# Graph attention kernel: steps of four single edge rows instead of two pairs, and landed data marked by VectorE

## The reference, cut to what matters

```python
x_l = (x @ W_l).reshape(n, 8, 16)
x_r = (x @ W_r).reshape(n, 8, 16)
e = (edge_attr @ W_e).reshape(-1, 8, 16)
m = leaky_relu(x_l[src] + x_r[dst] + e, 0.2)
alpha = einsum('ehc,hc->eh', m, att)
amax = segment_max(alpha, dst)
expa = exp(alpha - amax[dst])
denom = segment_sum(expa, dst)
out = segment_sum(x_l[src] * (expa / (denom[dst] + 1e-16))[:, :, None], dst)
```

## Time and profile before

| | |
|---|---|
| median of 3 runs | 2233.2 us (2232.06 to 2237.89) |
| the profiled execution's own time | 2248.54 us |
| its span | 2246.7 us |
| tables stage | 0 to about 52 us |
| gathers of the attention | 846.3 us to about 2126.5 us |
| last work of the attention | about 2185.2 us |
| granted TensorE clock, mean of the span | 0.864 |

### The profile page before, as it was taken

One profiled execution on the slowest core, in us unless ns is written; L12 is line 12 of the kernel. 1 busy time (PEld: TensorE's weight loads), 2 busy tenths in 40 slices (PEclk: granted clock), 3 DMA queues, 4 the chain that ended last, 5 costly groups with the idle time before them and its releaser, 6 DMA issues. The chain is left out here.

```text
span 2246.7 us, 35285 instructions
## 1 busy us (share of the span) xinstructions
PE 1820.9 (81%) x10692; PEld 1277.1 (57%) x10692; DVE 1327.8 (59%) x3113; ACT 1066.6 (47%) x2345; POOL 847.4 (38%) x891
## 2 busy tenths in 40 slices
PE   6777799979999973677878878878888778888776
PEld 2667665567888741345545555545555545555564
DVE  6999777664333363755555555555555555555585
ACT  1889867545423450234434444434444444444465
POOL 2000000010000016766666666666666666666500
PEclk9555599989999996799898998888989998999887
DMA  3000000005300012323233223323233233323311
GB/s 104 24 2 1 8 2 1 5 25 151 91 1 6 1 44 69 90 77 82 77 80 83 78 80 82 82 76 84 77 81 81 77 81 82 83 76 82 79 35 29
DMA packets 132195, 133.01 MB, mean 59 GB/s; under 512 B 28888, under 2 KB 102063, under 8 KB 132015
## 3 DMA queue, kind: packets, MB, share of 16 engines
q1 hardware_dynamic: 104238, 73.55, 11.4%
q0 software_dynamic: 27776, 57.20, 10.3%
HBM read 125.84 MB, written 4.82 MB: 58 GB/s over the span
## 5 line engine op out<-in xcount | busy, mean ns | idle before, releaser
L2275 POOL DMA_INDIRECT rows<-x_l,src x856 | 821.3, 959 | 477.1 <-issue 224.3
L2400 ACT ACTIVATE bent<-psum 128x512 f32<-128x512 f32 x214 | 127.4, 596 | 606.6 <-DMA near<-e_ends 340.6
L2361 PE MATMUL psum<-both,node_hot 128*128 128x144 f32 x1712 | 308.6, 323 | 66.3 <-issue 56.0
L2361 PEld LDWEIGHTS psum<-both,node_hot 128*128 128x128 f32 x1712 | 265.9, 213 | 143.0 <-issue 127.2
L2548 DVE TENSOR_TENSOR acc<-acc,psum 128x144 f32 x428 | 127.0, 297 | 278.4 <-remote 198.3
L2293 PEld LDWEIGHTS psum<-hot,x_r_parts 128*128 x1284 | 133.5, 104 | 249.0 <-issue 228.6
L2293 PE MATMUL psum<-hot,x_r_parts 128*128 128x256 bf16 x1284 | 201.2, 296 | 90.3 <-DVE hot L2454 31.1
L2415 ACT ACTIVATE apart<-iota,rel 128x128 bf16<-128x128 f32 x856 | 270.6, 388 | 1.4 <-PE psum L2361 1.4
L2313 PE MATMUL psum<-bent,att_heads 128*128 128x512 f32 x428 | 244.7, 661 | 9.0 <-DVE bent L2458 6.1
L2296 PE MATMUL psum<-edges,w_e 128*128 128x512 f32 x428 | 239.5, 642 | 0.7 <-issue 0.7
L2458 DVE TENSOR_TENSOR bent<-psum,bent 128x512 f32<-128x512 f32 x214 | 146.9, 686 | 127.9 <-issue 117.8
(11 more groups left out here) (347 smaller groups left out, 2400.3 us busy)
## 6 DMA issues: line engine op xcount, KB each, us to landing
rel_row<-e_rel_rows SPq DMA_DIRECT2D x107, 256.0 KB
edges<-edge_t SPq DMA_DIRECT2D x428, 32.0 KB
rows<-x_l,src POOLq DMA_INDIRECT x856
edge_part<-edge_t SPq DMA_DIRECT2D x40, 320.0 KB, 3.1
new<-e_new_before SPq DMA_DIRECT2D x26, 64.0 KB
new<-e_new_behind SPq DMA_DIRECT2D x26, 64.0 KB
ht<-x SPq DMA_DIRECT2D x6, 256.0 KB, 2.8
x_l<-rows SPq DMA_DIRECT2D x4, 320.0 KB
```

Source lines behind the costliest of these rows:

```text
L2275: e.indirect_dma_start(rows[:, g % ring, j * ROW:(j + 1) * ROW], None, k.xl, bass.IndirectOffsetOnAxis(ap=src[:, at:at + 1], axis=0)).then ...
L2361: final = e.matmul(to, near_hot[:, at, j, :], both[:, at, j, :], start=j % 2 == 0, stop=j % 2 == 1)
```

## The change

A piece of work is one row of 128 edges, a group is four rows, each with its own block. A row that lies in two blocks is taken twice: (806 + 24) / 4, rounded up, = 208 groups.

```diff
-        self.groups = -(-(self.pairs + self.nb - 1) // 2)
+        self.groups = -(-(self.tiles + self.nb - 1) // 4)
...
-EDGE_SLOTS = 3
+EDGE_SLOTS = 6
```

TensorE, `begin`, `join`, `turn_weights` and `sum_rows`:

```diff
-                    for j in range(2):
-                        half = slice(j * 2 * P, (j + 1) * 2 * P)
+                    for j in range(4):
+                        quarter = slice(j * P, (j + 1) * P)
                         for q in range(3):
-                            e.matmul(z[:, half], ...blocks[j]..., hot[:, two, half], start=j + q == 0, stop=False)
-                    e.wait_ge(edge_here[g % edge_slots].sem, edge_here[g % edge_slots].at(edge_lap(g)))
+                            e.matmul(z[:, quarter], ...blocks[j]..., hot[:, two, quarter], start=j + q == 0, stop=False)
                     e.matmul(z, w_e[:, :], edges[:, g % edge_slots, :], ...).then_inc(*products.up())
...
-                    e.wait_ge(got[g % slots].sem, got[g % slots].at(4 * lap(g)))
+                    e.wait_ge(seen.sem, seen.at(g + 1))
...
-                    if b.i >= 2:
-                        e.wait_ge(weighted.sem, weighted.at(plan[b.i - 2].over))
-                        e.wait_ge(filled.sem, filled.at(plan[b.i - 2].over))
+                    if b.i:
+                        e.wait_ge(weighted.sem, weighted.at(plan[b.i - 1].over))
+                        e.wait_ge(filled.sem, filled.at(plan[b.i - 1].over))
...
                     for j in range(4):
-                        to = bank[:, j // 2 * wide:(j // 2 + 1) * wide]
-                        final = e.matmul(to, near_hot[:, at, j, :], both[:, at, j, :], start=j % 2 == 0, stop=j % 2 == 1)
+                        row = 4 * u + j
+                        m, third = divmod(row, 3)
+                        bank = sum_banks[m % 3]
+                        if m >= 3 and third == 0:
+                            e.wait_ge(added.sem, added.at(adds(3 * m - 7)))
+                        ...
+                        final = e.matmul(bank[:, third * wide:(third + 1) * wide], near_hot[:, at, j, :], both[:, at, j, :],
+                                         start=True, stop=True)
```

SP and GpSimd:

```diff
-                        e.wait_ge(products.sem, products.at(g - edge_slots + 1))
-                    for j, at in enumerate(two):
-                        e.dma_start(...two rows of edge features...)
+                        e.wait_ge(leaky.sem, leaky.at(g - edge_slots + 1))
+                    for j, at in enumerate(four):
+                        e.dma_start(...one row of edge features...)
...
-                        e.wait_ge(joined.sem, joined.at(g - slots + 1))
+                        e.wait_ge(seen.sem, seen.at(g - slots + 1))
```

VectorE (`see(t + 1)` stands right behind `one_hots(t + 2)`; `see(0)` ahead of the loop):

```diff
                 def one_hots(g):
+                    e.wait_ge(edge_here[g % edge_slots].sem, edge_here[g % edge_slots].at(edge_lap(g)))
...
+                def see(g):
+                    e.wait_ge(got[g % slots].sem, got[g % slots].at(4 * lap(g)))
+                    e.tensor_copy(spot[:, g % 2:g % 2 + 1], rows_at(g)[:, 0:1]).then_inc(*seen.up())
...
-                    for j, to in enumerate(blocks):
-                        e.wait_ge(added.sem, added.at(adds(u) - 2 + j))
-                        e.tensor_tensor(to, to, bank[:, j * wide:(j + 1) * wide], ALU.add).then_inc(*added.up())
+                    for m in trios(u):
+                        bank = sum_banks[m % 3]
+                        e.wait_ge(totals.sem, totals.at(u + 1))
+                        for row in range(3 * m, min(3 * m + 3, 4 * groups)):
+                            to = acc[...the row's block...]
+                            ...
+                            e.wait_ge(added.sem, added.at(adds(row) - 1))
+                            e.tensor_tensor(to, to, bank[:, row % 3 * wide:(row % 3 + 1) * wide], ALU.add).then_inc(*added.up())
```

More of the change, by code:

```diff
@@ L537, in tables @@
         new_ready, stored = k.flag("new_ready"), k.flag("stored")
[L539 to L540 removed]
+        turns = [(srct, 0, 4, srcf), (relt, 0, 4, rel), (srct, 4, en, srcf), (relt, 4, en, rel)]
+        assert 4 < en <= 8 and len(c_cuts(s)) == 4
         ends_of = [(rowf, pair), (rows3, trio)]
         def turn(e, i):
[L544 to L546 removed]
+            _, lo, hi, of = turns[i]
+            for q in range(lo, hi):
+                last = e.transpose(k.bank[i][:, (q - lo) * P:(q - lo + 1) * P], of[:, q, :], k.ident[:, :])
             last.then_inc(*turned.up())
         def move(e, i):
[L550 removed]
+            to, lo, hi, _ = turns[i]
             e.wait_ge(turned.sem, turned.at(i + 1))
[L552 removed]
+            e.activation(to[:, lo * P:hi * P], k.bank[i][:, 0:(hi - lo) * P], ACT.Copy).then_inc(*moved.up())
         def turn_ends(e, i):
@@ L570, in _ @@
                 ended = groups.ends_of_tiles(e, v, c)
+                groups.find(e, v, c, ended, range(3))
                 c.vector_dst(e)
-                groups.vector(e, v, c, ended)
+                groups.find(e, v, c, ended, range(3, en))
+                groups.vector(e, v, c)
                 c.vector_src(e)
@@ L2139, in batch_of, with adds, trios @@
         return next(b for b in plan if b.first <= g < b.over)
-    def adds(u):
-        return 2 * (u + 1) + sum(b.first <= u for b in plan)
+    def adds(row):
+        return row + 1 + 2 * sum(4 * b.first <= row for b in plan)
+    def trios(u):
+        return [m for m in range(-(-4 * groups // 3)) if min(3 * m + 2, 4 * groups - 1) // 4 == u]
     def new_rows(b):
@@ L2205, in rows_at, with factors_in @@
             return rows[:, g % ring, :]
+        def factors_in(bank):
+            return bank[:, 3 * wide:3 * wide + HEADS]
         def weight_bank(b):
-            return k.bank[4 + b.two]
+            return k.bank[4]
         def turned_of(u):
@@ L2359, in sum_rows @@
                     for j in range(4):
-                        to = bank[:, j // 2 * wide:(j // 2 + 1) * wide]
-                        final = e.matmul(to, near_hot[:, at, j, :], both[:, at, j, :], start=j % 2 == 0, stop=j % 2 == 1)
+                        row = 4 * u + j
[3 more added lines that the diff above has]
+                            e.wait_ge(added.sem, added.at(adds(3 * m - 7)))
+                        if j == 0 and u in begun:
+                            i = begun[u].i
+                            e.wait_ge(spread.sem, spread.at(3 * i + 3))
+                            e.matmul(factors_in(bank), is_first[:, :], factor[:, :], start=True, stop=False)
+                            e.matmul(factors_in(bank), others[:, :], ones[:, :], start=False, stop=True).then_inc(*factors.up())
+                        final = e.matmul(bank[:, third * wide:(third + 1) * wide], near_hot[:, at, j, :], both[:, at, j, :],
+                                         start=True, stop=True)
                     final.then_inc(*totals.up())
                 e.wait_ge(loaded.sem, loaded.at(here))
-                block_of = Registers(k, ENGINE.PE, regs[0:1, 1, :], 2 * groups, s.nb - 1)
+                block_of = Registers(k, ENGINE.PE, regs[0:1, 1, :], 4 * groups, s.nb - 1)
                 begin(0)
@@ L2578, in _ @@
                 one_hots(1)
+                see(0)
                 def pieces(t, some):
@@ L2600, in _ @@
                         one_hots(t + 2)
+                    if t + 1 < groups:
+                        see(t + 1)
                     if t + 1 < cuts:
```

143 lines of the change are left out of this document (69 added, 74 removed).

## The result

The changed kernel takes 2525.62 us (median of 4 runs, 2520.41 to 2531.14), the kernel before 2234.78 us beside it: ratio 1.1299, interval 1.1272 to 1.1326. The prediction was 2082 us, range 1998 to 2270.

A forecast was written before the change was run, and what follows sets the result against it. It took late TensorE signals, binding both DMA-issuing engines, to set the attention's pace. From the profiled 2248.5 us, 157 less for the gathers, 3 more for the end and 2.5 for the tables gave 2097, scaled to 2082 us; range 1998 to 2270.

The forecast's parts named there:

- if the signals are prompt, the stops go: Attention gathers: GpSimd's wait moved to VectorE ends its 2 us stops; 5.40 us a group, 157 us less with fewer groups.
- Rival B: Attention: signals stay late, GpSimd restarts behind VectorE's queue, 1.53 us later at 100 stops, +153 us; 2355 us, chance 0.21.
- older piece of work: Argument against slower restarts: VectorE's copy runs one group ahead of the join, so GpSimd's wait may already be met.
- rival C: Attention gathers: GpSimd's floor of 5.06 us a group sets the pace, 227 us less; 2013 us, chance within the forecast's 0.52.
- TensorE: Attention: TensorE sets the pace at 5.28 us a group, including 0.66 for begin's twelve products.
- the theory of the signals: Attention: late TensorE signals, to which both DMA-issuing engines are bound, set the pace; moving the waits makes them prompt.
- Tables: Tables stage: SP's nine additional DMAs cost +2.5 us, from 0 to 7.6.
- End: After the last group: ten short steps follow instead of nine, +3 us.
- SP: Attention: two DMAs more a group stay hidden; without cover 1.2 us a group.
- the bank of weights: Attention: one bank makes turn_weights wait for the last weigh of the batch before; 0 to 28 us, taken as 0.
- factors: Attention: three banks of sums, factors of 8 columns, one additional VectorE operation a batch; 0, within 8 us either way.
- first steps: Attention's start: begin needs split x_r parts up to three steps earlier; 0 to 12 us, taken as 0.

The follow-up runs named there:

- e5: The changed kernel itself, unaltered, beside the kernel before, without late signals: 2022.9 us, ratio 0.993.
- e7: Kernel before, begin's six products of 256 columns made twelve of 128, four edge DMAs a group instead of two; not late: 2036.5 us, ratio 0.999.
- e1: Changed kernel with only GpSimd's wait undone, on TensorE's joined again; without late signals: 2021.1 us, kernel before 2039.6.
- e15: Changed kernel with all moved waits of GpSimd, SP and TensorE undone and no copy on VectorE; late signals: 2245.7 us, ratio 1.005.
- e10: Kernel before, GpSimd waiting for VectorE's copy, join held until the gathers six groups ahead land; late signals: 2713.8 us, ratio 1.207.
- e9: Kernel before, join in every second step held until the gathers five groups ahead land; late signals: 2427.6 us, ratio 1.080.
- the pause: A memset of 128 columns on GpSimd behind each gather: kernel before 2110.1 to 2115.1 us, changed kernel 2096.3 and, on joined, 2095.2 us.
- held kernels: Kernels before and changed, join made to wait for the landing of gathers five or six groups ahead: 2414.6 to 2813.9 us.
- e16: Changed kernel, GpSimd on joined again, join in every second step held for gathers five groups ahead; late signals: 2414.6 us, ratio 1.081.

## Why the prediction was wrong

**Failed: "if the signals are prompt, the stops go".** The term of the sum was 157 us less for the gathers, at 5.40 us a group without stops; measured are 245 us more, at 7.34 us a group with 106 stops of 4.66 us. The forecast took it that late signals come from who waits for whom, from one stage where neither held. The changed kernel has these waits of GpSimd, SP and TensorE moved, and 88 of its 201 slopes that start before the last gather still start more than 0.3 us after both join and ScalarE's own work are done (160 of 208 before; counted from the records of both lines). e5, e7 and e1 have none, be the waits moved (e5) or not (e7). So neither order of waits makes the signals late or prompt. How many are late does hang on it: with all waits undone (e15) it is 196 of 203. I had read the lateness as the program's own, and it is the occasion's: the tables' prompt signals were shown, but not that the attention's lateness came from the kernel at all.

Nor do the signals always wait for GpSimd to stand still, as I had read it. Of the 160 late slopes of before 104 start in a stop, but 54 over 1 us after the last restart, between gathers. The next one after the earlier trace rows is such a case: its join ended at 1504.46, and GpSimd was gathering again.

```profile
1507.38 0.94 POOL L2275 DMA_INDIRECT rows<-x_l,src  x1 [0.30 <-issue]
...
1507.88 0.60 ACT L2400 ACTIVATE bent<-psum 128x512 f32<-128x512 f32 x1 [2.12 <-DMA w<-L_gnn_W_self_t]
```

**Rival B was right in its mechanism, and mis-sized.** GpSimd's restart hangs behind VectorE's queue. B's term was slope 0.60, bend 0.68, one-hot 0.34, copy 0.16, less the 0.25 us that the restart takes today: 1.53 us later at each of 100 stops. Measured: 4.66 - 1.98 = 2.68 us at 106. Two things were wrong in the term. The 0.25 us were not to be taken off, for GpSimd still starts 0.27 us behind the copy (1526.33 to 1526.60). And the additions were left out, which stand ahead of bend: in the stop shown the first starts 0.76 us behind the burst and bend 2.27 us behind it, when the slope had long been done (1523.65). The other stops are alike. From 960 us on there are 85 in which a late slope starts; GpSimd restarts 3.46 us behind it in the mean (0.24 before), 2.18 of them lie ahead of bend, and bend waits for the slope in only 2. The remaining stops are shorter, hence the mean of 2.68. In e10, where few additions come between, the restart is 1.9 us behind the slope, 1.7 more than in e9: near B's term. What I held against B was wrong too: `see(t + 1)` stands behind `bend(t)`, which waits for the late join of t, so its "older piece of work" is not reached.

**The sum, in the condition without late signals.** There it is rival C's that holds: 208 groups at GpSimd's floor, 1053 us for the gathers against 1054.8 measured. But the kernel before runs at that floor too (e7, with the pairs, 1081.8 us for 214), so that the gain is 27 us there, not 227, and 14.5 us remain in the whole.

**TensorE.** I took 5.28 us a group and feared begin's twelve products. In e5 they take 0.83 us from the first start to the last end, as the six of 256 columns did (0.82): my 0.66 us were 0, the lower bound, and the 0.97 us that the prediction had as the other figure for the twelve was too much as well. TensorE kept up with 5.07. Its mean clock did not rise a little in the result but fell, from 0.864 to 0.816.

**Tables** +1.0 us instead of +2.5 (first gather at 847.3 instead of 846.3). **End:** from TensorE's last product of join to its last of `sum_rows` 49.8 us instead of 36.0 in the result's runs, 49.4 instead of 39.4 in e5 against e7: +10 to +14, not +3. With late signals GpSimd also ends one group further ahead: six joins start behind the last gather instead of five, and the last one ends 31 us behind it instead of 22. **SP, the bank of weights, factors, first steps:** with e7 at 0.999 and e15 at 1.005 none of them shows.

**The view that would have warned me** is the earlier trace rows itself: GpSimd restarts 0.24 us behind the burst and VectorE's bend 0.7 us behind it. Whatever makes the burst late, the change puts the second ahead of the first. The price of the moved wait was in the trace, whether or not the theory of the signals held; I gave it 0.21.

**Open.** What makes the signals late, and whether a lower rate of gathers lets them through: the pause met no late signal in five runs. The held kernels bear on it: in the condition with late signals, but with a stop at nearly every group, only 27 of 208 slopes are late in e9 and 33 of 202 in e16. That does not part a lower rate from standing still. Whether GpSimd's wait makes all of the 280 us or SP's and TensorE's have a part: the kernel with GpSimd's alone undone met no late signal in four runs. Held, it takes 8% over the kernel before (e16), as the kernel before itself does (e9), with SP's and TensorE's waits still moved, which speaks against a part of theirs. No version was found that beats the kernel before in both conditions; the changed one with GpSimd on joined is 0.6 to 1% faster without late signals and was not met with them, that with all waits undone 0.5% slower with them.

## What to carry to other kernels

A wait that is moved to another engine takes on everything that stands ahead of it in that engine's queue, and all that this waits for: read the order of the queue at the slowest moment, not at the usual one, and price the chain from burst to restart. An engine that sets the pace should wait for the signal that comes first, and directly. And a mechanism that the trace shows only in one execution's condition is a bet: before building on it, look for what does not depend on it.

## What the runs showed of the hardware

**The same program on the same kind of chip takes 2039 or 2235 us**, and the change's sign hangs on which. Nearly all that differs is the attention's gathers: with late signals the kernel before gathers for 1280 us, and nearly the same program without them (e7) for 1082, which is 198 of the 208 us between their spans. The first gather starts between 842.7 and 850.0 us in all twenty traces.

**Where TensorE's signals are late, SP's instructions are slow too.** The move of a register, which waits for nothing (ns min/median/max), in before, after, e15 (late) and e5 (not late):

```profile
L2237 SPq MOVE edges<-edge_t x428: 2/29/712, 844.9 to 2134.1; - x143
```

```profile
L2254 SPq MOVE edges<-edge_t x832: 2/29/719, 845.8 to 2379.0; - x167
```

```profile
L2254 SPq MOVE edges<-edge_t x832: 2/16/715, 847.4 to 2099.9; - x167
```

```profile
L2254 SPq MOVE edges<-edge_t x832: 29/29/43, 847.8 to 1882.7; - x167
```

A move of 29 ns can take 0.7 us, the same step in which TensorE's products crawl in the changed kernel (two of L2378, ahead of the stop shown, start at 1520.74 and 1521.46). Such moves show from one trace which condition it was taken in: the longest took 711 to 1408 ns in all seven traces with late signals, and 43 ns in all thirteen without. The register instructions of VectorE and TensorE are not slowed (at most 65 and 79 ns from 860 to 1850 us, in all twenty), nor do DMA packets take longer: from 950 to 1850 us those of the gathers' queue 119 to 133 ns in the mean in either condition. What slows SP's is not shown.
